# An expert item as one half of the features for two sequences, with one down projection per two items

## The reference

```python
X = X + ctx @ wo
h2 = rmsnorm(X, norm2_w).reshape(B * S, d)
logits = h2 @ router_w
...                                        # softmax, top 2 of 8, weights -> combine
shared = swiglu(h2, sh_gate, sh_up, sh_down)
gate = jnp.einsum('td,edf->etf', h2, e_gate)
up = jnp.einsum('td,edf->etf', h2, e_up)
eout = jnp.einsum('etf,efd->etd', jax.nn.silu(gate) * up, e_down)
spec = jnp.einsum('etd,te->td', eout, combine)
return X + (shared + spec)
```

## Time and profile before

| | us |
|---|---|
| median of 3 runs | 221.26 |
| lowest, highest | 218.88, 221.61 |
| profiled execution, its own time | 220.48 |
| its span, first to last instruction | 218.6 |
| TensorE busy in the span | 193.9 |
| VectorE busy | 139.4 |
| ScalarE busy | 106.8 |
| GpSimd busy | 54.6 |

### The profile page before, as it was taken

One profiled execution on the slowest core, in us unless ns is written; L12 is line 12 of the kernel. 1 busy time (PEld: TensorE's weight loads), 2 busy tenths in 40 slices (PEclk: granted clock), 3 DMA queues, 4 the chain that ended last, 5 costly groups with the idle time before them and its releaser, 6 DMA issues.

```text
span 218.6 us, 4395 instructions
## 1 busy us (share of the span) xinstructions
PE 193.9 (89%) x1575; PEld 167.1 (76%) x1575; DVE 139.4 (64%) x357; ACT 106.8 (49%) x215; POOL 54.6 (25%) x88
## 2 busy tenths in 40 slices
PE   7388995997888979879898989988999999999994
PEld 5265764874866757657686859978999999999993
DVE  2604667789596766857774765889665564554653
ACT  2636374665477757958788734324222223223220
POOL 2917396122010075216841034300000000000000
PEclk9959999999999999999999999999999999999999
DMA  5941993055457935793200000000000000000000
GB/s 139 234 128 22 160 163 42 17 69 69 69 70 94 139 108 70 86 132 103 78 0 0 3 0 0 3 0 1 17 10 3 0 25 3 0 3 24 0 4 24
DMA packets 8998, 11.55 MB, mean 53 GB/s; under 512 B 976, under 2 KB 6992, under 8 KB 8752
## 3 DMA queue, kind: packets, MB, share of 16 engines
q1 hardware_dynamic: 8976, 11.27, 29.1%
HBM read 5.50 MB, written 0.52 MB: 28 GB/s over the span
## 4 chain that ended last, share of the span: by engine, by line
PE 76%; DVE 14%; ACT 4%; issue 3%; POOL 1%; DVEq 0%; POOLq 0%; ACTq 0%
PE bank L1117 14%; PE bank L1106 7%; PE bank L1105 7%; PE bank L1107 7%; PE bank L1088 7%; PE bank L1062 6%; PE bank L1073 5%; DVE mxs L849 4%; PE bank L939 4%; PE bank L954 3%; PE bank L1126 2%; PE bank L930 2%; ACT k_st L519 2%; PE bank L1010 1%; PE bank L946 1%
## 5 line engine op out<-in xcount | busy, mean ns | idle before, releaser
L849 DVE TENSOR_REDUCE mxs<-bank 128x2 f32<-128x512 f32 x64 | 41.4, 687 | 15.2 <-PE bank L1062 14.8
L637 ACT ACTIVATE ep<-bank 128x512 f32<-128x512 f32 x64 | 36.5, 605 | 14.1 <-PE bank L1073 13.6
L1105 PE MATMUL bank<-split,whi 128*128 128x256 f32 x144 | 43.2, 300 | 0.0
L1106 PE MATMUL bank<-split,whi 128*128 128x256 f32 x144 | 40.7, 283 | 0.0
L1107 PE MATMUL bank<-split,wlo 128*128 128x256 f32 x144 | 40.2, 279 | 0.0
L1117 PE MATMUL bank<-down_s,early 128*128 128x128 f32 x288 | 38.3, 276 | 2.1 <-DVE early L866 2.0
L657 ACT ACTIVATE early<-bank 128x512 f32<-128x512 f32 x28 | 16.7, 598 | 46.9 <-PE bank L1107 46.9
L1117 PEld LDWEIGHTS bank<-down_s,early 128*128 128x128 f32 x288 | 35.0, 191 | 2.6 <-DVE early L866 2.2
L869 DVE TENSOR_TENSOR early<-early,bank 128x512 f32<-128x512 f32 x28 | 19.3, 688 | 25.4 <-PE bank L1107 25.3
L1062 PE MATMUL bank<-k_st,q_st 80*128 80x256 f32 x128 | 29.7, 317 | 0.9 <-DVE mxs L849 0.5
L1105 PEld LDWEIGHTS bank<-split,whi 128*128 128x128 f32 x144 | 27.3, 190 | 0.0
(11 more groups left out here) (141 smaller groups left out, 274.2 us busy)
## 6 DMA issues: line engine op xcount, KB each, us to landing
raw<-expert_w SPq DMA_DIRECT2D x9, 256.0 KB, 8.2
k_st<-k_st SPq DMA_DIRECT2D x7, 256.0 KB, 5.8
q_st<-split SPq DMA_DIRECT2D x24, 64.0 KB
k_st<-split SPq DMA_DIRECT2D x24, 64.0 KB
down_s<-expert_w SPq DMA_DIRECT2D x9, 128.0 KB, 8.0
early<-ctx_T SPq DMA_DIRECT2D x1, 672.0 KB, 9.3
xs<-x_tiles SPq DMA_DIRECT2D x2, 256.0 KB, 4.8
out_dram<-x SPq DMA_DIRECT2D x4, 128.0 KB, 1.8
```

The lines of the kernel that those rows point to most:

```text
L637: nc.scalar.activation(ep[:, n % NEP].rearrange("p t s -> p (t s)"), b_of(("exp", n))[:], ACT.Exp, scale=SCALE_H).then_inc(free(("exp", n) ...
L849: nc.vector.tensor_reduce(mxs[:, half % 2, :, 64 + h:65 + h], b_of(("max", n))[:].rearrange("p (t s) -> p t s", t=TB), AX_X, ALU.max).then ...
L1105: pe.matmul(bank, whi[:, fs], h2hi[:, hs], start=True, stop=False)
L1106: pe.matmul(bank, whi[:, fs], h2lo[:, hs], start=False, stop=False)
```

## The change

An item becomes one half (128 of 256 features) of one network for two sequences (512 tokens): six matmuls of 512 columns. Two items of a network then share one down projection of eight matmuls (16 records), which stands behind the up of the item after them. There are again 36 items. `act_t` gets four buffers instead of two. An item needs `h2` of both its sequences, and the output of two sequences is stored at once. The hand-written list is rearranged: some steps of the opening, slots of `SEQ_STEPS`, the weight splits, and the places of the first eight items (now slots 74, 75, 102, 106, 106, 119, 129 and 132).

```diff
--- before.py
+++ after.py
@@ -32,24 +32,24 @@
 NSTACK = 3
 SEQ_STEPS = {
     0: [("mT0", 9, 9), ("mT1", 17, 17), ("uT0", 30, 31), ("uT1", 31, 31), ("cT", 32, 32),
-        ("wo", 36, 39), ("square", 38, 41), ("h2", 38, 42), ("h2T", 46, 46), ("router", 54, 54)],
+        ("wo", 36, 39), ("square", 38, 41), ("h2", 39, 42), ("h2T", 46, 46), ("router", 54, 56)],
     1: [("mT0", 7, 7), ("mT1", 16, 17), ("uT0", 31, 31), ("uT1", 31, 31), ("cT", 31, 31),
         ("wo", 34, 34), ("square", 39, 39), ("h2", 39, 41), ("h2T", 44, 45), ("router", 47, 50),
-        ("route_exp1", 47, 51), ("route_top", 49, 52), ("route_exp2", 52, 56),
+        ("route_exp1", 47, 51), ("route_top", 49, 54), ("route_exp2", 52, 56),
         ("route_weights", 50, 58)],
-    2: [("mT0", 8, 8), ("mT1", 15, 15), ("uT0", 31, 34), ("uT1", 34, 35), ("cT", 35, 35),
-        ("wo", 40, 41), ("square", 41, 43), ("h2", 46, 49), ("h2T", 57, 60), ("router", 62, 66)],
-    3: [("mT0", 7, 9), ("mT1", 15, 15), ("uT0", 34, 36), ("uT1", 35, 42), ("cT", 41, 49),
-        ("wo", 47, 51), ("square", 51, 54), ("h2", 52, 55), ("h2T", 58, 60), ("router", 60, 62),
-        ("route_exp1", 66, 71), ("route_top", 66, 73), ("route_exp2", 75, 75),
-        ("route_weights", 90, 90)],
+    2: [("mT0", 8, 10), ("mT1", 15, 15), ("uT0", 31, 34), ("uT1", 34, 35), ("cT", 35, 35),
+        ("wo", 40, 41), ("square", 40, 44), ("h2", 46, 49), ("h2T", 57, 60), ("router", 62, 66)],
+    3: [("mT0", 7, 9), ("mT1", 15, 15), ("uT0", 34, 36), ("uT1", 35, 42), ("cT", 42, 50),
+        ("wo", 48, 52), ("square", 52, 56), ("h2", 53, 56), ("h2T", 59, 61), ("router", 62, 64),
+        ("route_exp1", 68, 72), ("route_top", 68, 75), ("route_exp2", 77, 77),
+        ("route_weights", 90, 91)],
 }
-FIRST_STEPS = """f0 g0 xn0 f1 t0 f2 q0 s0 g1 s1 p0 xn1 z0 g2 xn2 p1 q1 o0 o1 s2 s3 f3 q2 p2 j0 p3 n0 s4 o2 h0 o3
-                 p4 k0 n1 g3 e0 xn3""".split()
-MIXED_STEPS = {0: "h1", 1: "m0 s5", 2: "k1 e1 o4", 3: "p5 q3", 4: "e2 o5 e3 w0", 6: "s6", 7: "s7 n2 h2",
-               11: "p6 m1", 12: "k2 o6", 13: "p7 o7", 14: "w1 m2", 17: "n3 h3", 26: "m3", 28: "m4 k3", 38: "c3",
-               42: "m5 m6", 43: "m7 w2", 54: "w3", 71: "m8", 74: "i0", 75: "i0", 100: "i0", 102: "i0", 106: "i0",
-               111: "i0", 132: "i0 i0"}
+FIRST_STEPS = """f0 g0 xn0 q0 f1 f2 s0 g1 s1 t0 xn1 g2 p0 z0 xn2 p1 q1 o0 s2 s3 o1 f3 q2 p2 j0 p3 n0 s4 h0 o2 o3
+                 k0 g3 p4 e0 n1""".split()
+MIXED_STEPS = {0: "h1", 1: "s5", 2: "k1 m0 xn3 o4 e1", 3: "w0 p5 q3", 4: "e2 o5 e3", 6: "s6", 7: "s7 n2 h2 m1",
+               11: "p6", 12: "k2 o6 p7", 13: "o7", 14: "w1", 15: "m2", 17: "n3 h3", 21: "m3", 27: "k3", 32: "m4",
+               38: "c3 w2", 42: "m5 m6", 43: "m7", 52: "w3", 70: "m8", 74: "i0", 75: "i0", 102: "i0",
+               106: "i0 i0", 119: "i0", 129: "i0", 132: "i0"}
 BANKS = {"turn": (0, 1, 6), "proj": (2, 3, 7), "sum": (4, 5), "misc": (4, 5)}
 ITEMS = []
 WARM = 11
@@ -103,9 +103,8 @@
     SLOTS_A = max(read_at) + 1
 
 
-    dense = [(0, 0), (0, 1)] + [(e, b) for b in range(2) for e in range(1, NEXP)]
-    dense += [(e, b) for b in range(2, NB) for e in range(NEXP)]
-    dense = [dense[n] for n in ITEMS] if ITEMS else dense
+
+    dense = [(e, g, k) for g in range(NB // 2) for e in range(NEXP) for k in range(2)]
     ND = len(dense)
 
     order = [step_of(text) for text in FIRST_STEPS]
@@ -114,7 +113,7 @@
 
     def item(n):
 
-        return [("up", n)] + ([("down", n - 1)] if n else [])
+        return [("up", n)] + ([("down", n - 1)] if n and n % 2 == 0 else [])
 
     for i in range(SLOTS_A):
         order.append(("a", i))
@@ -206,7 +205,7 @@
         probs = early[:, 2 * NB * LK:2 * NB * LK + 2 * LK].rearrange("p (n k) -> p n k", n=2)
         probsT = early[:, 2 * NB * LK + 2 * LK:].rearrange("p (n c t) -> p n c t", n=2, c=KC)
         silu = early[:, 0:2 * 2 * L].rearrange("p (n f) -> p n f", n=2)
-        act_t = early[:, 4 * L:8 * L].rearrange("p (n f) -> p n f", n=2)
+        act_t = early[:, 4 * L:12 * L].rearrange("p (n f) -> p n f", n=4)
         qT = sb("qT", [P, NB, L])
         xnT = sb("xnT", [D, NB, L])
         bn6 = sb("bn6", [P, 2, NT, 6])
@@ -349,7 +348,7 @@
             for e in range(5, NEXP):
                 load_expert(sp, e)
             for b in range(NB):
-                is_read(sp, ("down", max(n for n, it in enumerate(dense) if it[1] == b)))
+                is_read(sp, ("down", max(n for n, it in enumerate(dense) if it[1] == b // 2)))
                 sp.dma_start(out[:, TB * b:TB * (b + 1)], x1[:, TB * b:TB * (b + 1)]).then_inc(out_stored, 16)
             sp.wait_ge(out_stored, 16 * NB)
 
@@ -853,15 +852,15 @@
                     misc(kind, b)
 
             def dense_up(n):
-                gated, up, out_t = silu[:, n % 2], ("up", n), act_t[:, n % 2]
+                gated, up, out_t = silu[:, n % 2], ("up", n), act_t[:, n % 4]
                 if n in tanh_items:
                     dve.wait_ge(tanh_ready, tanh_items.index(n) + 1)
                     nc.vector.scalar_tensor_tensor(out=gated, in0=gated, scalar=1.0, in1=b_of(("gate", n))[:],
                                                    op0=ALU.add, op1=ALU.mult).then_inc(free(("gate", n)), 1)
                 is_read(dve, ("gate", n))
                 is_full(dve, up)
-                if n >= 2:
-                    is_full(dve, ("down", n - 2))
+                if n >= 4 and n % 2 == 0:
+                    is_full(dve, ("down", n - 3))
                 if n in tanh_items:
                     nc.vector.scalar_tensor_tensor(out=out_t, in0=gated, scalar=0.5, in1=b_of(up)[:],
                                                    op0=ALU.mult, op1=ALU.mult).then_inc(free(up), 1)
@@ -869,10 +868,10 @@
                     nc.vector.tensor_tensor(out_t, gated, b_of(up)[:], ALU.mult).then_inc(free(up), 1)
 
             def dense_down(n):
-                e, b = dense[n]
+                e, g, _ = dense[n]
                 is_full(dve, ("down", n))
-                for j in range(TB):
-                    i = TB * b + j
+                for j in range(2 * TB):
+                    i = 2 * TB * g + j
                     c = tg[:, 1:2] if e == 0 else cw[:, i, e - 1:e]
                     last = nc.vector.scalar_tensor_tensor(out=x1[:, i, :], in0=b_of(("down", n))[:, j * D:(j + 1) * D],
                                                           scalar=c, in1=x1[:, i, :], op0=ALU.mult, op1=ALU.add)
@@ -1093,29 +1092,27 @@
                     misc(step, b)
 
             def dense_up(n):
-                e, b = dense[n]
+                e, g, k = dense[n]
                 pe.wait_ge(w_split, e + 1)
-                pe.wait_ge(h2s_ready, b + 1)
-                hs = slice(b * L, (b + 1) * L)
+                pe.wait_ge(h2s_ready, 2 * g + 2)
+                hs = slice(2 * g * L, (2 * g + 2) * L)
                 for i, use in ((0, ("gate", n)), (1, ("up", n))):
                     may_fill(pe, use)
-                    for k in range(2):
-                        bank = b_of(use)[:, k * L:(k + 1) * L]
-                        fs = slice(((2 * e + i) * 2 + k) * P, ((2 * e + i) * 2 + k + 1) * P)
-                        pe.matmul(bank, whi[:, fs], h2hi[:, hs], start=True, stop=False)
-                        pe.matmul(bank, whi[:, fs], h2lo[:, hs], start=False, stop=False)
-                        last = pe.matmul(bank, wlo[:, fs], h2hi[:, hs], start=False, stop=True)
-                    last.then_inc(full(use), 1)
+                    bank = b_of(use)[:]
+                    fs = slice(((2 * e + i) * 2 + k) * P, ((2 * e + i) * 2 + k + 1) * P)
+                    pe.matmul(bank, whi[:, fs], h2hi[:, hs], start=True, stop=False)
+                    pe.matmul(bank, whi[:, fs], h2lo[:, hs], start=False, stop=False)
+                    pe.matmul(bank, wlo[:, fs], h2hi[:, hs], start=False, stop=True).then_inc(full(use), 1)
 
             def dense_down(n):
-                e, b = dense[n]
+                e, _, _ = dense[n]
                 is_read(pe, ("up", n))
                 pe.wait_ge(ld_down[e], 16)
                 may_fill(pe, ("down", n))
-                for j in range(TB):
+                for j in range(2 * TB):
                     for f in range(2):
                         last = pe.matmul(b_of(("down", n))[:, j * D:(j + 1) * D],
-                                         act_t[:, n % 2, f * L + j * P:f * L + (j + 1) * P],
+                                         act_t[:, (n - 1 + f) % 4, j * P:(j + 1) * P],
                                          down_s[:, f, e * D:(e + 1) * D], start=(f == 0), stop=(f == 1))
                 last.then_inc(full(("down", n)), 1)
```

## The result

| | before | after |
|---|---|---|
| median of 4 runs each, us | 220.44 | 228.44 |
| lowest, highest | 218.88, 221.61 | 227.70, 230.09 |
| ratio after to before | | 1.0378, 95% interval 1.0284 to 1.0472 |
| profiled execution, own time | 220.48 | 228.31 |
| its span | 218.6 | 226.5 |

The forecast was 222.1 with a range to 225.4: too low by 6.3 us, and "same" where the answer is "slower".

What follows compares the result with a forecast made beforehand. TensorE's matmul queue was taken to bound the last 60 us, with the clock at 1.00; -2.3 + 1.85 + 2.35 - 0.3 = +1.6 us on 220.48 gave 222.1, range 218.6 to 225.4.

Steps and rivals of the forecast that it cites:

- pace of the 512-column matmuls: Feed-forward ups: six matmuls of 512 columns for twelve of 256 save half of 10.5 ns per matmul, -2.3 us.
- pairs wait in the steady stage: Steady feed-forward stage: a shared down following one up still finds its product ready, so cost nothing.
- tail: After the last up: a 16-record last down, its four accumulations and a second store issue, +1.85 us, ends 1.5 and 3.3.
- items among the slots, waits: Mixed attention stretch: longer stall behind routing, downs after only one up, no item before sequence 3's router; +2.35 us, ends 0 and 3.5.
- opening: Start of the kernel: sequence 1's second norm moves behind the first query stack, first score matmul earlier, -0.3 us.
- a wrong reading out of three: Extra per 512-column matmul: fixed (224 ns, taken), growing with columns (234 ns, saving 0) or vanishing (213 ns, saving 4.6 us).
- the deciding point: 512-column matmul pace: measuring above 229 ns decides for an extra that grows with the columns.
- the first rival: Feed-forward matmuls: the extra grows with the columns, 234 ns for 512, nothing saved, 224.4 us; chance 0.2.
- Rival 4: Mixed attention stretch does not stall more, only tail and pace count: 219.8 us; chance 0.14.
- Cost nothing: Opening: GpSimd's 2.6 us of memsets move behind the first bias additions, where it idled 4.32 us; ends -1.1 and +2.6.
- the 0.23 us to spare: Steady stage: the product, queued behind four accumulations, still fits before its down with 0.23 us left.
- rival 3: Steady stage: each down one up after its item waits, 13 x 0.25 = 3.3 us, giving 225.4 us; chance 0.1.

Runs made afterwards that it cites:

- old_lists: The kernel after with the opening and attention lists of before, item form and item slots new: 223.85 us, ratio 1.0093 to before.
- mt0_back: The kernel after with mT0 of sequence 2 put back two slots earlier on ScalarE's list, as before: 225.60 us, ratio 1.0196 to before.
- opening_only: The kernel before with the new opening list and the steps of slots 0 to 4 of after: 224.72 us, ratio 1.0174 to before.
- cols_256: The kernel after with each 512-column matmul issued as two of 256, pairs of downs kept: 228.22 us, ratio 1.0324 to before.
- slots_only: The kernel before with the SEQ_STEPS of after and nothing else: 223.59 us, ratio 1.0122 to before.
- old_slots: The kernel of old_lists with its first eight items at the slots of before: 221.95 us, ratio 1.0118 to before.
- short_routing: The kernel after with VectorE's small routing steps for sequences 2 and 3 cut from 15 to 3: 225.68 us, ratio 1.0182 to before.
- tail_halves: The kernel of old_lists with the last down in two banks, each with its own signal: 223.12 us, ratio 1.0145 to before.
- norm_back: The kernel after with VectorE's second norm of sequence 1 back at its old place in the opening: 231.0 us (226.95 to 232.19), no ratio.
- cols_384_128: The kernel after with each 512-column matmul as one of 384 and one of 128, run once: 236.68 us.

## Why the prediction was wrong

| term of the sum | predicted | measured |
|---|---|---|
| pace of the 512-column matmuls | -2.3 | -0.7 |
| pairs wait in the steady stage | 0 | 0 |
| tail | +1.85 | +1.7 |
| items among the slots, waits | +2.35 | +1.25 |
| opening | -0.3 | about 0 |
| other moved slots, as waits | not costed | +1.3 |
| granted clock | not costed | +5.1 |

The measured column adds up to 8.65; the start of the first score matmul was 1.0 us earlier, of which old_lists, with the opening of before, shows 0.9 (35.82) as scatter from one execution to the next. The difference of the spans is 7.9; the 0.25 left are waits too short to list, and rounding.

**The step that failed most: no term for the clock.** The prediction read 1.00 in both stretches and took it as given. The trace of before shows one wait of 2.00 us without a fall, so nothing there said that a wait of 2.16 would be followed by one. But the same trace has a low stretch at its wait of 4.24 us in the opening, and the runs spread from 218.88 to 221.61 for one program: something outside of the rows moved by 1%, and a change with more and longer waits was the one to push it. The runs show in place of the clock of 1.00 three stretches at 0.50, 1.7 us each. mt0_back shows for the one at 95 us that with the wait gone the low clock is gone, in line with the count of 7 and 10 profiles above; opening_only shows that the one at 54 comes with the new opening; the one at 156 comes with the new items (8 of 8 profiles with the wait, against 1 of 5 with the old ones).

**The step that was left out: the moved slots.** The prediction costed the items and the opening line by line, and passed over SEQ_STEPS and the rest of MIXED_STEPS. The diff shows `("mT0", 8, 8)` becoming `("mT0", 8, 10)`. On ScalarE two exps of 0.6 us, at TensorE's rhythm, then stand ahead of a copy of 1.0 us, and the score matmul of that sequence waits for it: a term of about a microsecond was there to be found. Together with the low clock behind it it is worth 2.8 us (mt0_back). All lists together are worth 4.6 by the medians (after less old_lists), where the whole item form with its slots is worth 2.6 (old_lists less before).

**Pace: a wrong reading out of three.** The prediction took 10.5 ns as fixed per matmul and put the deciding point at 229 ns for 512 columns. It measured 232.5, and 4.57 us for a pair where 4.47 was forecast: the first rival. Two items took 4.61 us before and take 4.57 now, 0.04 x 18 = 0.7 us; cols_256, with the rest of the kernel unchanged, has 4.62, so the part that is fixed per matmul is 4 ns and not 10.5. The row that misled was the opening's 0.43 us for 512 columns at 1.2 GHz: 0.84 ns a column there, 0.446 at 2.4 GHz, so the step in clock did not halve the time exactly, and a row at one level did not carry over to the other. (The clock column has 1.00 at that place; the spacing of 0.43 us is what shows the 1.2 GHz.) The Trainium skill ("TensorE: Matmul & The Clock Gate", Back-to-back issue gap) gives 216 ns for 512 columns; this case's trace disagrees by 16.5 ns.

**Items among the slots: mechanism right, size too large, form incomplete.** The router of sequence 3 waits 1.09 us where it did not wait before, against 0.85 reckoned. The size came out, the reason did not: the prediction had it wait for the copy of h2T, and the trace has it released by VectorE's four accumulations of down 3. It is there with the items of before too (0.94 in slots_only) and not in old_lists, so the moved steps of sequence 3 make it, not the items' slots. The wait at down 7 is 2.16 against a forecast of 3.1, hardly longer than before. The count from the end of up 5 (146.56) shows the two errors:

```profile
146.69 0.69 DVE L858 SCALAR_TENSOR_TENSOR early<-early,bank 128x512 f32<-128x512 f32 x1 [0.63 <-ACT early L654]
```

VectorE takes 8.5 us from there to the end of item 7's second product (155.11) and not 8.8; TensorE takes 6.3 us to the end of up 8's issue (152.83) and not 5.8, by the pace and because down 5 starts only behind item 5's product (148.15). Had TensorE not stood at the router it would have waited no longer: old_slots has no wait there and the same 2.17 at down 7. Downs 3 and 5 show no wait above 0.4 in after (0.82 at down 5 in old_lists). short_routing shows that the routing steps make the wait, 2.16 to 0.17. What was not foretold is the 1.7 us of low clock behind it. Rival 4, no more stall there, is false: 3.25 us at router and down 7 together against 2.00.

**Opening.** The norm was to leave the path and give 0.3 to 1.1. Moved, it runs beside GpSimd's bias addition and weight split, and its four instructions take 2.87 us for 1.23; the first score matmul came no earlier than in a kernel with the old opening (35.72 and 35.82, and 36.66 and 36.74). "Cost nothing" had named GpSimd's idle time, but not that VectorE's own instruction changes its length beside GpSimd. By the estimate above that costs 0.2 us at most; what the opening cost was the low stretch at 54 us.

**What was right.** The steady stage has no idle row, so the 0.23 us to spare held and rival 3 is false. The tail came out at +1.7, made of sixteen records, four accumulations and a second store; tail_halves gets 0.9 back. The stall after the routing stands where it was put, released by VectorE's product. The forecast's sum for the item form and its slots alone, +1.9 without the opening, lies within what old_lists measured (+2.6, interval of the ratio +0.7 to +3.4 us), but that is luck, through errors that partly cancel: the pace's gain too large by 1.6 and the half clock of 1.7 left out, against waits reckoned too long (2.35; in old_lists they are 0.56, 0.82 and 0.17 more at down 7).

**What stays open.** Which move of the new opening brings the low stretch at 54 us. The 1.40 us wait just before it is the same in both kernels, and from 42.2 to 53.8 us the two profiles agree within 0.03 us but for one step and its copy on ScalarE: `w0`, the value projection of sequence 0, moved from slot 4 to slot 3 and stands at 46.69 before and at 41.34 after, so that TensorE waits 0.76 us at 48.06 and not 0.32.

```profile
41.34 0.61 PE L991 MATMUL bank<-ffn_s,xnT 128*128 128x128 f32 x4
...
48.06 1.10 PE L938 MATMUL bank<-early,qT 97*128 97x512 f32 x2 [0.76 <-DVE q_st L764]
...
51.66 0.44 PE L961 MATMUL bank<-ident,xs 128*128 128x128 f32 x2 [1.40 <-DVE xs L733]
```

Whether these 0.44 us decide was not tried; norm_back, with the norm at its old place, has both waits and the low stretch, so it is not the norm. Nor did the edits that removed one low stretch always lower the sum: short_routing and norm_back show others elsewhere. So a wait is a condition that these runs bear out, no more; which of several alike is followed by the low clock wasn't found. That the wait alone, without the half clock, would have made the change "same" is arithmetic (7.9 - 5.1 = 2.8 us, 1.3%), not a run.

## What to carry to other kernels

Cost every entry of a hand-written order that a diff touches, also the small ones that read as noise: a step moved by two slots cost about as much here (2.8 us) as the new tiling of the whole feed-forward (2.6). Ask of each wait of over a microsecond on TensorE what follows if the clock falls behind it, and widen the range by that (1.7 us a place here), since the price of a wait can double. Wider matmuls of the same columns gain only the part of their time that is fixed per instruction; get that part from two widths at the same clock level, and look for the long wait in the opening first, where moving one 3.69 us cast gave 2.2%.

## What the runs showed of the hardware

- **Matmul spacing of this type at 2.4 GHz is nearly proportional to columns**: 118.3 ns at 256, 175 at 384, 232.5 at 512; at 128 columns 59 in one place of three and 112 in the other two (cols_384_128).
- **VectorE stretches beside GpSimd**: two instructions of 128x128 with two operands in memory of the core took 0.61 us alone and 1.18 to 1.69 beside GpSimd. The Trainium skill ("SBUF — State Buffer", SBUF: two separate sides) says that such an instruction and a GpSimd one that reads there exclude each other on a shared pair of ports, the later one waiting. The trace agrees: VectorE's 1.69 us lie over GpSimd's 1.27, and its 1.18 over the 0.72 and the 0.61; which engine held a port no row shows.
- **The granted clock differs between executions of one program**, 0.940 to 0.992 in 46, and with it the time, 229.8 to 217.8 us. Differences of under 1% need it beside the time: old_slots at 0.984 took 221.24 where before's median at that clock is 220.0.
- **The same wait of TensorE is or is not followed by a stretch at 1.2 GHz**: 7 of 7 waits of 1.27 to 1.28 us in one place were, and 4 of 5 of 2.00 to 2.74 in another were not. Such a stretch cost 1.7 us.
